# Token attention's results turned by VectorE out of SBUF, and Wo's rows loaded in the order that this leaves

## The reference

```python
x = x + 0.5 * ffn(layernorm(x))
x = x + attn(layernorm(x))          # 8 heads, softmax over 512 tokens
x = x + 0.5 * ffn(layernorm(x))

# ffn(x), H = 16 heads of HD = 16, E = 8 experts
h   = rmsnorm(x, gamma1)
q   = (h @ Wq + bq)                 # b t H HD
k,v = split((h @ Wdown + bdown) @ Wup + bup)
att = softmax(einsum('bthd,btgd->bthg', q, k) / 4)
out = einsum('bthg,btgd->bthd', att, v)      # each token attends over its own 16 heads
x   = x + (out.reshape(b, t, 256) @ Wo + bo)
h2  = rmsnorm(x, gamma2)
gate = softmax(h2 @ Wg + bg)
return x + einsum('btd,edf,bte->btf', h2, We, gate)
```

## Time and profile before

| | us |
|---|---|
| median of 3 runs | 1035.9 (1035.76 to 1036.86) |
| span of the profiled execution, first to last instruction | 1033.7 |
| what lies around the span, by the median | 2.2 |
| PE busy | 990.4 (96%) |
| DVE busy | 815.1 (79%) |
| POOL busy | 768.1 (74%) |
| ACT busy | 675.6 (65%) |

### The profile page before, as it was taken

How to read it: one execution, slowest core, us unless ns; L and a number is a source line. 1 busy time by engine, 2 the same in 40 slices (tenths; PEclk the granted TensorE clock), 3 DMA queues, 4 the chain that set the end, 5 groups by cost and what they waited for, 6 DMA issues and landing times.

```text
span 1033.7 us, 28419 instructions
## 1 busy us (share of the span) xinstructions
PE 990.4 (96%) x11328; PEld 778.7 (75%) x11328; DVE 815.1 (79%) x1236; ACT 675.6 (65%) x1411; POOL 768.1 (74%) x789
## 2 busy tenths in 40 slices
PE   7899999999999989999999999878999999999998
PEld 6688888888888866666666666557888888788886
DVE  7787777787785479999999999997777777776754
ACT  5777467475674458777778777676774675655742
POOL 7968778596674459889899899996686685865734
PEclk8999999999999999999999999999999999999999
DMA  6210000000000000000000000000000000000001
GB/s 207 74 42 3 2 2 1 2 3 1 3 2 1 2 1 2 2 2 1 2 1 3 2 2 2 2 1 2 3 22 2 23 2 22 22 2 22 22 2 41
DMA packets 7855, 14.22 MB, mean 14 GB/s; under 512 B 1833, under 2 KB 5548, under 8 KB 7726
## 3 DMA queue, kind: packets, MB, share of 16 engines
q1 hardware_dynamic: 7726, 12.41, 3.5%
HBM read 8.21 MB, written 4.19 MB: 12 GB/s over the span
## 4 chain that ended last, share of the span: by engine, by line
PE 81%; DVE 9%; POOL 4%; issue 4%; ACT 1%; DVEq 0%; POOLq 0%; ACTq 0%
PE psum L492 54%; PE psum L900 5%; PE psum L910 4%; PE psum L926 4%; PE psum L665 3%; PE psum L676 3%; DVE oT L1197 3%; DVE late L1203 3%; PE psum L811 2%; POOL kvx L1591 1%; PE psum L802 1%; PE psum L826 1%; PE psum L792 1%; PE psum L752 1%; POOL late L1591 1%
## 5 line engine op out<-in xcount | busy, mean ns | idle before, releaser
L492 PE MATMUL psum<-we,h 128*128 128x512 f32 x1536 | 393.5, 401 | 0.0
L492 PEld LDWEIGHTS psum<-we,h 128*128 128x128 f32 x1536 | 277.4, 188 | 59.2 <-issue 0.2
L1171 DVE SCALAR_TENSOR_TENSOR X<-psum,gate,X 128x256 f32<-128x256 f32 x260 | 125.1, 481 | 60.0 <-PE psum L492 50.4
L1549 POOL TENSOR_TENSOR late<-late 128x512 f32<-128x512 f32 x63 | 81.3, 1290 | 121.9 <-ACT late L1345 121.9
L1407 ACT ACTIVATE kvx<-psum 128x1024 f32<-128x1024 f32 x126 | 129.1, 1025 | 62.4 <-PE psum L910 60.8
L1197 DVE TENSOR_REDUCE oT<-psum 128x128 fp32r<-128x1024 f32 x128 | 154.4, 1217 | 15.2 <-PE psum L900 14.7
L1345 ACT ACTIVATE late<-psum,gate 128x256 f32<-128x256 f32 x252 | 104.4, 465 | 89.4 <-PE psum L492 54.6
L1203 DVE TENSOR_REDUCE late<-kvx 128x256 f32<-128x2048 f32 x63 | 143.3, 2275 | 0.2 <-POOL late L1591 0.2
L1591 POOL TENSOR_TENSOR kvx<-kvx,late 128x2048 f32<-128x2048 f32 x32 | 125.3, 3915 | 16.4 <-ACT late L1414 16.4
L1591 POOL TENSOR_TENSOR late<-kvx,late 128x2048 f32<-128x2048 f32 x31 | 122.1, 3938 | 19.9 <-ACT late L1414 19.9
L1266 ACT ACTIVATE kvx<-kvcs,mask 128x512 f32<-128x512 f32 x132 | 86.3, 728 | 27.8 <-DVE kvcs L1071 25.5
(11 more groups left out here) (171 smaller groups left out, 1972.8 us busy)
## 6 DMA issues: line engine op xcount, KB each, us to landing
X<-in_L_attn_hidden_states SPq DMA_DIRECT2D x8, 512.0 KB, 4.9
out<-X SPq DMA_DIRECT2D x7, 512.0 KB, 2.6
X<-in_L_ffn_We SPq DMA_DIRECT2D x2, 1024.0 KB, 10.0
out<-X SPq DMA_DIRECT2D x1, 384.0 KB, 2.3
kvx<-in_L_ffn_Wq SPq DMA_DIRECT2D x1, 256.0 KB, 3.0
kvx<-in_L_ffn_Wup SPq DMA_DIRECT2D x2, 128.0 KB, 2.7
kvx<-in_L_ffn_Wo SPq DMA_DIRECT2D x1, 256.0 KB, 4.1
X<-in_L_attn_Wk SPq DMA_DIRECT2D x1, 256.0 KB, 3.0
```

Of the source, the lines that this page charges most:

```text
L492: ins = e.matmul(out_ap, l, r, start=(n == 0), stop=(n == len(terms) - 1))
L1171: e.scalar_tensor_tensor(out=xi, in0=psum[:, u % 3, w * D:(w + 1) * D], scalar=gate[k % 2][:, i, 2 * n + w:2 * n + w + 1], in1=xi, op0=ALU ...
L1549: own.step(e.tensor_tensor(y[:, 0:2, :], y[:, 0:2, :], y[:, 2:4, :], ALU.add))
```

## The change

The step `turn_out` (four transposes on PE, one bank of PSUM) is gone. `out_turn` reads `on` straight from SBUF: its 32x32 blocks now hold 32 tokens by the 32 rows of a partition group, read with a step of 16 elements, and come out with the channels in the order d * 16 + h in place of h * 16 + d. To match, `oT`'s transposes use another permutation matrix `perm` and write each of their four results as two runs of 64 columns, and `Wo` is loaded with its rows in that order, by eight transfers of 16 partitions in place of one of 128. `perm` is made by four copies of 32 columns where `swap` took one of 128. The list of steps changes with it: `attend` and `mult` of a pair wait for `mult` and `out_turn` of the pair before, and `out_turn` comes directly after `mult`, with an assumed 700 ns.

```diff
-RING = {..., "turn_probs": ("at",), "turn_out": ("out_turn",),
+RING = {..., "turn_probs": ("at",),
...
-            put("PE", 1085, ("attend", c), ("at", c), ("turn_out", c - 1))
-            put("DVE", 1000, ("mult", c), ("attend", c))
-            put("PE", 435, ("turn_out", c), ("mult", c), ("oT", s - 1, p))
-            put("DVE", 630, ("out_turn", c), ("turn_out", c))
+            put("PE", 1085, ("attend", c), ("at", c), ("mult", c - 1))
+            put("DVE", 1000, ("mult", c), ("attend", c), ("out_turn", c - 1))
+            put("DVE", 700, ("out_turn", c), ("mult", c), ("oT", s - 1, p))
...
-                elif name == "turn_out":
-                    c = piece[1]
-                    e.wait_ge(s_on, c + 1)
-                    for a4 in range(4):
-                        ins = e.transpose(psum[:, b, a4 * P:(a4 + 1) * P], on[:, a4 * P:(a4 + 1) * P], ident[:, :])
-                    ins.then_inc(s_onT, 1)
                 elif name == "oT":
...
+                    tokens = psum[:, b, :].rearrange("p (k i u n) -> p k u i n", k=KC, i=2, u=2)
                     for kk in range(KC):
-                        for i in range(2):
-                            ins = e.transpose(pair_bank(b)[:, kk, i * P:(i + 1) * P], ot[p][:, i, kk * P:(kk + 1) * P], swap[:, :])
+                        for u in range(2):
+                            ins = e.transpose(tokens[:, kk, u], ot[p][:, u, kk * P:(kk + 1) * P], perm[:, :])
...
-            e.tensor_copy(swap[:, :].rearrange("p (u n o) -> p u n o", u=2, o=2),
-                          ident[:, :].rearrange("p (o n u) -> p u n o", u=2, o=2)).then_inc(s_consts_dve, 1)
+            place = perm[:, :].rearrange("p (i l a j o) -> p i l a j o", i=2, l=2, a=4, j=4)
+            come = ident[:, :].rearrange("p (j a o l i) -> p i l a j o", j=4, a=4, l=2, i=2)
+            for i, l in product_of((0, 1), repeat=2):
+                ins = e.tensor_copy(place[:, i, l], come[:, i, l])
+            ins.then_inc(s_consts_dve, 1)
...
                     if c:
-                        e.wait_ge(s_onT, c)
-                        e.wait_ge(s_on, c)
+                        e.wait_ge(s_ot, c)
...
-                    e.wait_ge(s_onT, c + 1)
-                    src = psum[:, b, :].rearrange("p (r h) -> p h r", h=H)
-                    dst = ot[c % 2][:, :, :].rearrange("p b (h d) -> p h b d", h=H)
+                    e.wait_ge(s_on, c + 1)
+                    src = on.rearrange("p (t d) -> p d t", d=HD)
+                    dst = ot[c % 2][:, :, :].rearrange("p u (d h) -> p d u h", h=H)
                     e.transpose(dst, src).then_inc(s_ot, 1)
...
-            e.dma_start(raw_o, a["L0_ffn_Wo"].rearrange("(k c) n -> c k n", c=P)).then_inc(l_wo, 16)
+            for d in range(HD // KC):
+                e.dma_start(raw_o[d * H:(d + 1) * H],
+                            a["L0_ffn_Wo"].rearrange("(h k d) n -> d h k n", h=H, k=KC)[d]).then_inc(l_wo, 16)
```

More of the change, by code:

```diff
@@ L32 @@
           "gate", "gate_copy", "gateT", "gate_sub", "gate_exp", "gate_soft"}
-BY_PAIR = {"expand_P", "expand_A", "scores", "top", "exp", "turn_probs", "at", "attend", "mult", "turn_out", "out_turn"}
+BY_PAIR = {"expand_P", "expand_A", "scores", "top", "exp", "turn_probs", "at", "attend", "mult", "out_turn"}
 def attention_plan(B, NT, KC):
@@ L634, in freed_by @@
                 return s_on, c
-            if name == "turn_out":
-                return s_ot, c
             if name == "oT":
```

14 lines of the change are left out of this document (7 added, 7 removed).

## The result

The changed kernel takes 1039.1 us (median of 7 runs, 1037.6 to 1040.2) where the kernel before took 1036.2 beside it. The ratio is 1.0027, with a 95% interval of 1.0016 to 1.0038: slower by about 2.8 us. The prediction was 1028.1, faster by 7.8.

A forecast was written before the change was run, and what follows sets the result against it. PE was taken to bound the full stretches, with chains through ACT, DVE and POOL in the ramps; -8.8 (groups) + 0 (ramps) + 0.4 (copies) + 0.6 (late We) = -7.8 us, 1035.9 to 1028.1, range 1022.5 to 1032.5.

The forecast's parts named there:

- groups of `turn_out` gone, full stretches: PE, 120 to 340 and 790 to 1000 us: twenty groups of four transposes at 0.44 us, 8.8 us less.
- groups gone in the ramps, with `perm`'s copies: 0 to 120 and 640 to 790 us: ten groups, at most -4.4 us; three more DVE copies at the start, +0.4.
- waits of the new order: PE waits in the ramps behind chains on ACT and DVE; upper bound eats the groups and +4.4 us more.
- longer turn: DVE's turn out of SBUF: 0.72 us taken, 1.13 as upper bound, covered either way, so 0 us.
- eight issues of `Wo`: SP's queue at the start: seven more issues, 3.0 us, make We and pair 0's exponentials 0.6 us late; bounds 0 and 1.0.
- ramps: 0: 0 to 120 and 640 to 790 us: middle of bounds -4.4 and +4.4 us, so no net change.
- The full stretches' order: 120 to 340 and 790 to 1000 us: each block runs at PE's own speed; no cost for order counted.
- both end before PE is there, so the cover holds for either: Full stretches: mult and turn take 1.8 or 2.2 us, PE reaches oT 2.8 us after attend, so no stall.
- The rule that the prediction set against itself: DVE's turn: SBUF reads 64 bytes apart exceed 0.72 us by an ungiven price; at 1.13 the sum stays the same.
- The copies of `perm`: Start, DVE: four copies for one make the first statistics 0.4 us late; bounds 0 and 0.5.
- Slower: Third rival, chance 0.05: turn from SBUF far longer, by step or waiting for POOL; decides from 1.7 us, about +29, 1065.
- Rival 2: Ramps and start take most back: +3 for the new order's waits, +1.3 for late We, -8.8; 1031.4 us, chance 0.15.

The follow-up runs named there:

- e6: Changed kernel with Wo in one transfer, the order of the kernel before, and the turn reading unbroken runs (output not the reference's): 1025.0 us, ratio 0.9898.
- e4: Changed kernel with Wo in one transfer and every engine in the order of the kernel before, turn_out struck out: 1029.1 us, ratio 0.9929.
- e1: Changed kernel with only Wo's load put back to one transfer, its new order and turn kept: 1036.0 us, ratio 1.0001.
- e12: Changed kernel with Wo in one transfer, its new order up to pair 6 of the first block, the old order after: 1033.1 us, ratio 0.9972.
- e16: Changed kernel, Wo in one transfer, new order up to pair 6, pair 0's gap filled with 14 transposes, job 0's half moved behind kv_turn: 1028.9 us, ratio 0.9925.
- e3: Changed kernel with Wo in one transfer, new order, and the turn reading SBUF in unbroken runs: 1032.0 us, ratio 0.9962.
- e2: Kernel before with only Wo's load changed, to the eight transfers of the changed kernel: 1038.2 us, ratio 1.0023.
- e5: Changed kernel with Wo in two transfers over 128 partitions and the order of the kernel before; computes the reference: 1030.0 us, ratio 0.9938.
- e13: Changed kernel with Wo in one transfer, its new order only up to pair 1, the old order after: 1033.7 us, ratio 0.9979.
- e17: Changed kernel, Wo in one transfer, new order up to pair 6, job 0's half moved behind kv_turn, gap not filled: 1031.7 us, ratio 0.9959.

## Why the prediction was wrong

The prediction's terms, beside what the runs give for the same thing (ratios times 1036):

| term | predicted | measured | from |
|---|---|---|---|
| groups of `turn_out` gone, full stretches | -8.8 | about -10 | e6, distances of the gates |
| groups gone in the ramps, with `perm`'s copies | -4.4 + 0.4 | about -0.5 | what is left of e6's -10.6 |
| waits of the new order | +4.4 | +7.5 | e4 to e1 |
| longer turn | 0 | +3.2 | e6 to e4 |
| eight issues of `Wo` | +0.6 | +2.7 | e1 to the change |
| sum | -7.8 | +2.8 | |

The term "ramps: 0" is split here into its two parts: at the middle of its bounds, -4.4 for ten groups and +4.4 for the new order's waits. No single step explains the miss of 10.6 us. Four terms are off by 2.1 to 3.5 us each, all in the same direction: the groups and the waits in the ramps, the turn, and the eight issues. The term for the full stretches held, and gave some 1 us more than was taken.

- **The groups** ("twenty groups at 0.44 us are 8.8 us less", and 4.4 more in the ramps). The price is right in the full stretches: with the old order and the flat turn a job gains 0.90 us, where 0.88 were taken. In the changed kernel the longer turn and the new order leave 0.52 and 0.30 of it. In the ramps the price is wrong: ten groups bring next to nothing there even in the old order, since PE waits for other engines where they stood. The prediction had said of the ramps that PE "waits for chains through ACT, DVE and POOL", but put their groups in at the full 0.44 us.
- **The order in the ramps** ("the bounds are that all ten groups come off (-4.4), and that the new order's waits eat them and as much again (+4.4); I take the middle, 0"). This step failed: 6.5 us of waits with a gain of about 0.5 from the groups is some +6, outside the upper bound. The middle of two bounds was no estimate. The prediction found the gap behind `attend` of pair 0, at the right place: it said 2.0 us of idle time on PE, and it is 2.4. But it then had `scores` of pair 1 at 36.4, 1.0 us late, and it starts at 39.95 in e1 (by the distance from the exponentials, 2.95 us later than before, and 1.5 us in e12, where the clock stayed up). Two things behind the gap were missed. The granted clock can fall to its lower level, so that `q` takes 2.9 us and not 1.7; that happened in some profiles of both orders and not in others. And on DVE the new order puts `half` and `x1` ahead of the lower half of `la`, for which PE waits next. Removing both brings 4.9 us in the first ramp (e12 to e16), either alone no more than can be told from noise.
- **The full stretches' order.** Taken at nothing; it costs 1 to 3 us by the times, and by the distances of the gates 0.15 us a job in the first block and 0.4 in the second.
- **The turn.** 1.08 us lay within the prediction's bounds (0.72 to 1.13), and nearly at the upper one. The step that failed is "both end before PE is there, so the cover holds for either". The wait at `oT` does stay small in mid-block (none from 120 to 340 us), and yet the 0.37 us cost 0.10 to 0.13 us a turn in the whole, and 0.2 to 0.4 us a job in mid-block (40.53 to 40.31 from e1 to e3, 40.77 to 40.41 in the second block). They are on DVE's own line 32 times, ahead of its other steps; through which of these PE comes later isn't shown. The rule that the prediction set against itself (the Trainium skill, "Advanced Engine Details and Errata", section Memory Cachelines: full speed in SBUF only where successive accesses share a line of 16 bytes) agrees with the trace: 0.71 us for unbroken runs, 1.08 for steps of 64 bytes. How wide the line is no run tests.
- **The eight issues.** The step "seven more are 1.8 to 3.1 us, and I take 3.0" failed, and its upper bound with it: an issue of a 16-partition piece took 0.63 us, more than that of the whole 128 partitions (0.44). SP was 4.6 us late, and the second half of `We` was there at 28.05 us, where the transfers of before had ended at 22.0 and 25.0 was forecast. So ACT's exponentials were 3.6 us late and not 0.6, above the bound of 1.0, which had itself been worked out from a shift of 3.4 us, more than the 3.1 allowed for (2.7 us late in e2, where nothing but the load differs). That cost 2.4 to 2.7 us.
- **The copies of `perm`.** Right: the first statistics start at 4.65 where they started at 4.41, 0.2 us late instead of the 0.4 taken.
- **The rivals.** "Slower" came true, but not by its mechanism: the turn shows no wait for POOL (its 32 lengths lie within 61 ns), and 1.08 us is far from the 1.7 us from which it was to decide. Rival 2 named the right causes ("the new order's waits in both ramps", "We later than I think") at 3 and 1.3 us, where they are 6.5 and 2.7, and the turn was missing from it.

**What stays open.** The 2 us of the second ramp and the 1 to 3 us of the full stretches and ends were placed, not traced to a wait, and so were the last 1.2 to 1.4 us at job 1's product with `Wup`. After the same idle time of PE in the same order the clock stayed up in one profile and fell in another; what tells them apart is not shown. What a fall costs in the end isn't shown either, so of the four causes in my theory the clock is not shown as one of its own. In the old order it puts job 1's product with `Wup` 1.1 us back (e4 to e5, by the distance from the exponentials). But the mean granted clock of the kernel before differs between its executions, from 0.994 to 1.000, and in the five groups the 44 with 0.997 or less have a mean span of 1033.3 us, the 53 others 1034.9; an earlier start can go with the lower clock, which these figures don't part. That another order alone costs 7.7 us in the kernel before shows that an order's fit is worth about as much as the change itself, and doesn't tell why the order of before is the better.

## What to carry to other kernels

When a change removes a step from a list that a scheduler turns into a fixed order, test it with the old order first, with the step struck out: with `Wo` in one transfer, that alone parted a gain of 7 us from none. Count a removed step at its price only in stretches where its engine never waits: here the groups brought their 0.44 us there, and next to nothing in the ramps. Price what is added on an engine that is "a quarter idle" by whom its later steps serve, not by whether the next reader waits. Read a fall of TensorE's clock in more than one profile before it is charged to an order. When two waits follow each other, try both repairs together, since either alone may bring nothing that can be told from noise. Count each DMA that is issued ahead of a late load by a measured issue of a piece of that shape, and keep a permuted load to a few transfers over all partitions: two cost nothing measurable, eight cost 2.4 to 2.7 us.

## What the runs showed of the hardware

- **Reading SBUF with a step on VectorE.** The blockwise transpose of 128x512 numbers took 1.08 us (1.045 to 1.106) out of SBUF in steps of 64 bytes and 0.711 in unbroken runs. Out of PSUM with the same step it took 0.716: the step that costs 0.37 us in the one memory shows no such cost in the other. No run reads PSUM in unbroken runs.
- **What an issue on SP takes.** 0.63 us for 16 partitions of 2 runs each, 0.66 for 128 partitions at half the columns (1.32 for two), both with the rows of the source in another order, and 0.44 for the whole in one with the rows as they lie. So the width in partitions alone doesn't decide it. That the cut of the source does is my reading; no run separates them.
- **VectorE and POOL both reading SBUF.** An instruction of 0.68 us with two inputs in SBUF lasted 3.19 us in one profile and 3.21 in another beside POOL's subtractions. The Trainium skill states the cause in "SBUF — State Buffer", section "Who interferes with whom": a VectorE instruction with two inputs in SBUF contends with a GpSimd instruction that reads SBUF. The trace agrees, and shows how long it can last: it didn't get in between POOL's four subtractions of some 1.25 us each, and ended 0.5 us behind the POOL instruction that followed them. In e13 it started later and lasted 1.23, and there POOL's next instruction was the longer one, 1.04 instead of 0.62.
- **The clock.** TensorE had done nothing for 2.88 us in the changed kernel, and the granted clock then was 0.50, the lower level, for 12 us. Behind 2.09 us of idle time in the old order it stayed at 1.00 in e4 and fell to 0.50 in e5 and e6; behind 2.37 and 2.38 it stayed at 1.00 in e12 and fell in e1, e13 and e17. In e16 it fell with only 0.71 us of idle time just before (0.71 from 28 to 30 us, 0.50 from 30 to 32). Twelve matmuls of 256 columns took 1.66 us at the upper level and 2.90 at the lower. Filling such a gap with transposes that nobody reads brought 1.3 to 3.5 us, of which only the 3.5, together with the moved step, is clear of noise.
